# Decoder layer on one core: how PSUM banks are shared between row maxima and scores in self attention, and where a group's last transposition stands

## What is computed

```python
Qt = einsum('bqhf,hfg->bqhg', Q, W_cross);  scores_cross = Qt . K
scores_conv = Q . (K mixed by shift_weights)
scores = (gt * scores_cross + (1 - gt) * scores_conv) * hd ** -0.5
attn = softmax(where(causal, scores, -inf))
x = x + (attn . V) @ Wo.T + bo
x = x + cross_attention(layernorm(x), ctx, ctx, mask)
x = x + (silu(h @ Wg.T) * (h @ Wu.T)) @ Wd.T      # h = layernorm(x)
```

## Time and profile before

| | us |
|---|---|
| median of 3 runs | 1120.48 (1118.62 to 1124.39) |
| the profiled execution | 1129.87 |
| its span | 1128.1 |
| TensorE busy in the span | 1045.1 (93%) |
| VectorE busy | 741.7 (66%) |
| ScalarE busy | 562.6 (50%) |
| GpSimd busy | 222.3 (20%) |

### The profile page before, as it was taken

How to read it: one execution, slowest core, us unless ns; L and a number is a source line. 1 busy time by engine, 2 the same in 40 slices (tenths; PEclk the granted TensorE clock), 3 DMA queues, 4 the chain that set the end, 5 groups by cost and what they waited for, 6 DMA issues and landing times. The chain is left out here.

```text
span 1128.1 us, 19085 instructions
## 1 busy us (share of the span) xinstructions
PE 1045.1 (93%) x7044; PEld 620.4 (55%) x7092; DVE 741.7 (66%) x1603; ACT 562.6 (50%) x1061; POOL 222.3 (20%) x199
## 2 busy tenths in 40 slices
PE   2888889999999999999999799899898899999997
PEld 2777434444444444444444366444443688888886
DVE  5999887777787778877885266555444555555552
ACT  1445146666666667666766458377655211111110
POOL 6545540000000000000000023201101133333331
PEclk9999779999999999999999899699968899999999
DMA  8259812333444444444400135687971211111101
GB/s 245 104 198 232 260 30 40 64 67 71 74 74 79 81 77 78 81 81 78 78 16 14 25 102 138 144 197 150 220 157 64 74 39 50 51 51 49 44 20 37
DMA packets 87827, 105.27 MB, mean 93 GB/s; under 512 B 14910, under 2 KB 76010, under 8 KB 86199
## 3 DMA queue, kind: packets, MB, share of 16 engines
q1 hardware_dynamic: 85239, 100.90, 38.4%
q10 hardware_dynamic: 2496, 3.16, 1.3%
HBM read 61.80 MB, written 37.06 MB: 88 GB/s over the span
## 5 line engine op out<-in xcount | busy, mean ns | idle before, releaser
L738 DVE TENSOR_REDUCE pm<-bank 128x1 f32<-128x512 f32 (+3 forms) x608 | 356.6, 653 | 87.5 <-PE bank L814 66.7
L786 ACT ACTIVATE prob<-bank 128x512 f32<-128x512 f32 (+1 forms) x608 | 317.4, 583 | 186.0 <-PE bank L830 99.1
L809 PE MATMUL bank<-stk,stq 96*128 96x512 bf16 (+3 forms) x768 | 227.4, 340 | 5.1 <-DVE pm L738 2.9
L826 PE MATMUL bank<-stq,stk 98*128 98x512 bf16 (+3 forms) x768 | 222.4, 330 | 2.6 <-ACT prob L786 0.5
L840 PE MATMUL bank<-prob,va 128*17 128x512 f32 (+3 forms) x1536 | 145.5, 497 | 2.5
L809 PEld LDWEIGHTS bank<-stk,stq 96*128 96x128 bf16 x768 | 68.8, 98 | 136.9 <-DVE pm L738 81.0
L1541 ACT ACTIVATE e_sg<-bank 128x512 f32<-128x512 f32 x48 | 28.7, 598 | 189.3 <-PE bank L135 189.3
L959 POOL TENSOR_TENSOR c_rstd<-c_ve,mhalf 128x4 f32<-128x4 f32 x8 | 8.1, 1011 | 504.9 <-DVE c_ve L128 504.9
L1296 ACT ACTIVATE xprob<-bank 80x512 f32<-80x512 f32 x128 | 72.5, 592 | 69.1 <-PE bank L1336 67.8
L826 PEld LDWEIGHTS bank<-stq,stk 98*128 98x128 bf16 x768 | 69.4, 99 | 44.9 <-ACT prob L786 9.2
L1258 DVE TENSOR_REDUCE xpm<-bank 128x4 f32<-128x320 f32 x128 | 59.0, 488 | 39.1 <-PE bank L1321 37.5
(11 more groups left out here) (172 smaller groups left out, 1403.8 us busy)
## 6 DMA issues: line engine op xcount, KB each, us to landing
qk<-a_parts SPq DMA_DIRECT2D x32, 384.0 KB, 4.4
od<-xu SPq DMA_DIRECT2D x16, 512.0 KB, 4.8
xq<-c_parts SPq DMA_DIRECT2D x16, 384.0 KB, 2.7
xstq<-xq SPq DMA_DIRECT2D x32, 192.0 KB, 4.6
stq<-qk SPq DMA_DIRECT2D x30, 192.0 KB, 4.0
stk<-qk SPq DMA_DIRECT2D x15, 384.0 KB, 6.5
vs<-a_vst SPq DMA_DIRECT2D x8, 544.0 KB, 4.7
oall<-u_out SPq DMA_DIRECT2D x64, 64.0 KB
```

Of the source, the lines that this page charges most:

```text
L738: nc.vector.tensor_reduce(pm[:, k, h0:h0 + hb, r], src[:, 0:hb * w].rearrange("p (h w) -> p h w", h=hb), AX, ALU.max).then_inc(s_mxe, 1)
L786: nc.scalar.activation(prob[:, U % NPS, 0:hb * n], bank[STB[U % NSB]][:, 0:hb * n], ACT.Exp).then_inc(s_ex, 1)
L809: mm = nc.tensor.matmul(dst[:, h * w:(h + 1) * w], stq[i][0:R, half, h0 + h, r * P:(r + 1) * P], stk[i][0:R, h0 + h, k0:k0 + w], start=(h ...
L826: mm = nc.tensor.matmul(dst[:, h * n:(h + 1) * n], stk[i][0:RM, h0 + h, kt * P:(kt + 1) * P], stq[i][0:RM, half, h0 + h, q0:q0 + n], start ...
```

## The change

Self attention now has four banks for maxima and two for scores. The plan is one running list `order` over all groups: the 38 maxima of a group with t0 behind the first four of the second half, as before, and t1 of group g behind the first two maxima of group g + 1 (`DEFER = 2`). Its 40 items per group are spread evenly over all 38 score units from unit 0. VectorE follows the same order. Cross attention keeps three and three banks under names of its own (`XMB`, `XSB`). The wait of TensorE at the end of the projections is one chunk part later, for the fourth bank.

```diff
-            t.wait_ge(s_r, 4 * (NCH - 1) + 1)
+            t.wait_ge(s_r, 4 * (NCH - 1) + NMB - 2)
...
-        ring = [("m", i) for i in range(len(mx_units))]
-        ring.insert(n_half + 4, ("t", 0))
-        ring.append(("t", 1))
-        NMX = len(ring)
-        NPS, LAG, LATE = 16, 3, 3
-        MXB, STB, PVB = (0, 1, 2), (3, 4, 5), (6, 7)
+        NPS, LAG, DEFER = 16, 3, 2
+        MXB, STB, PVB = (0, 1, 2, 3), (4, 5), (6, 7)
...
+        order, spell = [], []
+        for g in range(G):
+            spell.append(len(order))
+            for m in range(len(mx_units)):
+                if g and m == DEFER:
+                    order.append((g - 1, "t", 1))
+                if m == n_half + 4:
+                    order.append((g, "t", 0))
+                order.append((g, "m", m))
+        spell += [len(order), len(order) + 1]
+        order.append((G - 1, "t", 1))
...
-            if u == LATE:
-                plan.append(("r", NMX - 1, 0))
-            upto = max(0, u - LATE + 1) * (NMX - 1) // (NST - LATE)
-            plan += [("r", n, 1) for n in range(at, upto)]
-            at = upto
+            plan.append(("r", u, 0))
...
             for g in range(G):
-                item(g, NMX - 1)
-                if g + 1 < G:
-                    for n in range(NMX - 1):
-                        item(g + 1, n)
+                for N in range(spell[g + 1], spell[g + 2]):
+                    item(N)
...
-                    elif what == "r" and g + ahead < G:
-                        maxima(g + ahead, which)
+                    elif what == "r":
+                        if g == G - 1:
+                            due = range(todo if which == DEFER else 0)
+                        else:
+                            due = range(-(-which * todo // NST), -(-(which + 1) * todo // NST))
+                        for n in due:
+                            maxima(spell[g + 1] + n)
```

More of the change, by code:

```diff
@@ L606, in program @@
         joint_end = [sets[s - s % 2 + 1][3] for s in range(len(sets))]
-        ring = [("m", i) for i in range(len(mx_units))]
-        ring.insert(n_half + 4, ("t", 0))
-        ring.append(("t", 1))
-        NMX = len(ring)
-        NPS, LAG, LATE = 16, 3, 3
-        MXB, STB, PVB = (0, 1, 2), (3, 4, 5), (6, 7)
-        NMB, NSB = len(MXB), len(STB)
-        plan, at = [], 0
+        NPS, LAG, DEFER = 16, 3, 2
+        MXB, STB, PVB = (0, 1, 2, 3), (4, 5), (6, 7)
+        NMB, NSB = len(MXB), len(STB)
+        order, spell = [], []
[9 more added lines that the diff above has]
+        order.append((G - 1, "t", 1))
+        place = {item: n for n, item in enumerate(order)}
+        NMX = len(order)
+        plan = []
         for u in range(NST):
@@ L679, in maxima @@
             def maxima(g, c):
-                sp.wait_ge(s_mxe, g * NMX + ring.index(("t", c)) + 1)
+                sp.wait_ge(s_mxe, place[g, "t", c] + 1)
                 for t in range(2):
@@ L728, in self_vector, with item @@
         def self_vector(v, first):
-            def item(g, n):
-                kind, m = ring[n]
-                N = g * NMX + n
+            def item(N):
+                g, kind, m = order[N]
                 src = bank[MXB[N % NMB]]
@@ L755, in self_vector @@
             if first:
-                for n in range(NMX - 1):
-                    item(0, n)
+                for N in range(spell[1]):
+                    item(N)
                 return
             for g in range(G):
-                item(g, NMX - 1)
-                if g + 1 < G:
-                    for n in range(NMX - 1):
-                        item(g + 1, n)
+                for N in range(spell[g + 1], spell[g + 2]):
+                    item(N)
                 b = g // GB - 1
@@ L794, in self_tensor, with maxima @@
         def self_tensor(t, first):
-            def maxima(g, n):
-                i, N = g % NB, g * NMX + n
-                kind, m = ring[n]
+            def maxima(N):
+                g, kind, m = order[N]
+                i = g % NB
                 dst = bank[MXB[N % NMB]]
-                if n == 0:
+                if kind == "m" and m == 0:
                     t.wait_ge(ld[i], 16 * NLD * (g // NB + 1))
@@ L845, in self_tensor @@
             if first:
-                for n in range(NMX - 1):
-                    maxima(0, n)
+                for N in range(spell[1]):
+                    maxima(N)
                 return
@@ L853, in self_tensor @@
             for g in range(G):
+                todo = spell[g + 2] - spell[g + 1]
                 for what, which, ahead in plan:
@@ L856, in self_tensor @@
                         if which == min(EARLY):
-                            t.wait_ge(s_mxe, G * NMX)
+                            t.wait_ge(s_mxe, NMX)
                         EARLY[which](t)
@@ L1114, in program @@
         ring2.append(("t", 1))
+        XMB, XSB = (0, 1, 2), (3, 4, 5)
+        NXM, NXS = len(XMB), len(XSB)
         NMX2, NST2, NPS2, LAG2, AHEAD, LATE2 = len(ring2), 2 * HG, 8, 3, 2, 2
@@ L1251, in item @@
                 N = g * NMX2 + n
-                src = bank[MXB[N % NMB]]
+                src = bank[XMB[N % NXM]]
                 v.wait_ge(xs_mxf, N + 1)
@@ L1295, in cross_scalar @@
                     need(a, xs_pv, U + 1 - NPS2)
-                    nc.scalar.activation(xprob[:, U % NPS2], bank[STB[U % NSB]][0:SK, :], ACT.Exp).then_inc(xs_ex, 1)
+                    nc.scalar.activation(xprob[:, U % NPS2], bank[XSB[U % NXS]][0:SK, :], ACT.Exp).then_inc(xs_ex, 1)
                     if u == NST2 - 1:
@@ L1308, in maxima @@
                 kind, m = ring2[n]
-                dst = bank[MXB[N % NMB]]
+                dst = bank[XMB[N % NXM]]
                 if n == 0:
                     t.wait_ge(xld[i], 32 * len(Q_RUNS) * (b + 1))
-                need(t, xs_mxe, N + 1 - NMB)
+                need(t, xs_mxe, N + 1 - NXM)
                 if kind == "t":
@@ L1328, in scores @@
                     t.wait_ge(xmd[g % 2][half], 32 * (g // 2 + 1))
-                need(t, xs_ex, U + 1 - NSB)
-                dst = bank[STB[U % NSB]]
+                need(t, xs_ex, U + 1 - NXS)
+                dst = bank[XSB[U % NXS]]
                 q = slice(half * 512, half * 512 + 512)
```

## The result

The changed kernel takes 1159.47 us (median of 4 runs, 1155.47 to 1169.93) against 1119.98 for the kernel before in the same series: 1.036 times as long, 95% interval 1.029 to 1.044, so 39.5 us slower. The forecast was 1146.0, slower, with a range up to 1162.

What follows compares the result with a forecast made beforehand. TensorE was taken to bound self attention. 15 groups x (2.2 + 0.2 - 0.9) = +22.5, last group +3.4 and start -0.4 give +25.5 us on the median 1120.5: 1146.0 us, range 1128 to 1162.

Steps and rivals of the forecast that it cites:

- Scores wait for ScalarE: Self attention: with two banks a score waits for the exponential of the score two before; 2.2 us a group added.
- the walk: Unit-by-unit reckoning of score starts and exponential ends between bursts of products in a group; it gave 2.2 us a group.
- t1 waits 0.2 us: Self attention: t1 behind two maxima waits for VectorE's last reduction and parts; 0.2 us a group, ends 0 and 0.5.
- The maxima's waits go: Self attention: a fourth bank removes TensorE's waits for VectorE's reductions; 0.9 us a group gained, ends 0 and 4.3.
- The last group: Last group of self attention: ScalarE's pace rules and long TensorE pieces begin with two filled banks; +3.4 us.
- The start: First maxima, bounded by VectorE: a fourth bank saves some 0.4 us; t1 of group 0 still waits.
- The sum: Whole kernel: 15 groups at +1.5 us, the last group and the start together give +25.5 us.
- Faster: the maxima were the real wait: Rival for self attention: maxima's waits vanish and scores don't wait; 1110 us, chance 0.07.
- Little changes: Rival for self attention: the score bank comes free early, 0.9 us a group lost and 0.9 gained; 1126.5 us, chance 0.14.
- The clock falls: Rival for self attention: TensorE's clock halves once a group, 51 us on top; 1197 us, chance 0.07.

Runs made afterwards that it cites:

- Short exponentials: The changed kernel with exponentials working on at most the first 256 columns of each tile, so part of the softmax is left out; one run, 1139.4 us.
- late copies: The changed kernel with ScalarE's two output copies moved behind units 10 and 21; 1146.5 us, 1.020 of the kernel before.
- t1 behind four: The changed kernel with t1 behind four maxima of the next group instead of two; 1154.5 us, 1.027 of the kernel before.
- banks alone: The kernel before, in its old order, with four banks for maxima and two for scores; 1153.1 us, 1.026 of the kernel before.

## Why the prediction was right, point by point

- **Scores wait for ScalarE** (2.2 us a group, 0.19 at unit 24, 0.51 at unit 19): right; 2.5 measured, 2.3 more than before, with 1.07 us from unit 22 to unit 24 as worked out. The small miss is at unit 16, whose wait behind t0 is 0.17 us instead of 0.10. Short exponentials show that the chain's length is the cause, late copies that the part for the output copies was rightly placed (0.68 expected by the walk, 0.69 measured).
- **t1 waits 0.2 us**: right; 0.24, and with t1 behind four it goes in all but every fourth group.
- **The maxima's waits go** (0.9 us a group): the mis-sized term. 0.6 went. What stays is 0.13 us in most groups and 0.9 in every fourth, where VectorE has the reciprocals of the denominators and what follows them in its queue ahead of the next reductions, 2.0 us, for longer than one more bank covers. The cause was only half right too. The fourth bank would do it alone (0.88 to 0.15 us with three score banks and one for products), but in the changed kernel the scores' waits do most of it, and the bank adds 0.13. That the size came out near is in part luck. In the timeline of group 6 after, where rows 6 show 0.62 us before the change:

```profile
345.92 0.22 PE L833 MATMUL bank<-tri_k,identb 128*128 128x128 bf16 x1
...
346.59 0.34 PE L812 MATMUL bank<-stk,stq 96*128 96x384 bf16 x1 [0.45 <-DVE pm L743]
```

  I had written that this one goes too; it is 0.67 us now.
- **The last group** (+3.4 us): right at full clock (31.2 to 34.7), and there some 0.5 of it is not the banks'. In the first profile it is +4.8, the rest by the clock. That the granted clock would be 1.0 all through self attention was wrong there: it is 0.87 in the last group of the first profile.
- **The start** (-0.4 us): t1 of group 0 comes 0.34 us earlier in that profile (151.92 instead of 152.26); a second profile of each (152.80 and 153.01) has it at 0.2. Within what the half-clock stretches there move.
- **The sum** (+25.5 us): too small. The profiled spans give 27.9: the 0.4 us a group above 1.5 add 6 us, and shorter later stages take 4 back. The second profiles give 32.6: 26.7 for 14 groups, 3.4 for the last, 1.1 up to t1 of group 1 and 1.4 behind. The medians give 39.5, and 36.4 beside the second four runs; some 5 us of the first are its low series of before. What is left of the 36.4 above 32.6, some 4 us, is not traced to a stage; the half-clock stretches in the last group, which four of the five profiles above have and that second one has not, would be of that size (37.1 to 38.9 us there instead of 34.7). The forecast of 1146.0 was 13.5 us low, and the measured time lies 2.5 us inside the upper end of the range; that end came from the ends of the terms, of which none was the clock or a low series, so that it holds the measured time is in part luck.
- **Rivals.** "Faster: the maxima were the real wait" falls with banks alone. "Little changes" supposed that a bank is free 0.49 us after the exponential's start; the 1.07 us rule it out. "The clock falls" did not happen between t1 of group 1 and t1 of group 15, where the granted clock is 1.00, as the rows of cross attention had suggested. So the trace does not bear out, for the 14 groups, the rule of the Trainium skill (TensorE: Matmul & The Clock Gate, A second HAM failure mode: psum-queue depth-cycling) that I weighed there. The clock does fall in the last group in some executions. Idle times of TensorE of 0.2 to 0.8 us follow each other there, but they are the same in the second profile of the changed kernel, at full clock, so they are not shown to be what lets it fall.

What stays open: why the last group has half-clock stretches in some executions and not in others (six of the eight profiles with the new order have them, one of the four with the old, so the order may matter), and why the stages behind self attention spend between 51 and 102 us at half clock from one profile to another. In banks alone, 19 us less of it went with stages 10 us shorter.

## What to carry to other kernels

Before taking a bank from a ring, add up the loop that it closes: stream, start of the reader, the reader's whole length, release. Here that is 1.07 us, and two banks serve it only where the producer brings two tiles in more than that; average busy shares (ScalarE: 20.6 of 30.0 us) say nothing about it. And look for a ring whose users never overlap, as the two product banks here, before trading between two that are both in use.

## What I had not expected of the hardware

A wait of TensorE of 0.2 us, as at unit 24, shows no idle time in the profile, since the modelled end of a 512-column matmul lies 0.16 us behind the next possible start: of the 2.5 us a group that scores wait for ScalarE (35 us in 14 groups), the profile's waits show 8.1 us as idle time of TensorE. And the half-clock share of one kernel differs between executions: 107 and 112 us in the two profiles of before, 109 and 124 in those of after, with equal time per group in self attention.
